# The 64-row last chunk of 704 gated values, filled with zeros to 128 rows in two feed-forward stages

## What is computed

```python
gate = jnp.einsum('bted,edf->btef', dispatched, gate_proj)
up = jnp.einsum('bted,edf->btef', dispatched, up_proj)
acts = jax.nn.silu(gate) * up                                  # 704 gated values
expert_out = jnp.einsum('btef,efd->bted', acts, down_proj)     # sum over 704
```

```python
gate = fp4_linear(x, w_gate)
y = fp4_linear(x, w_up)
h = jax.nn.silu(gate) * y
return fp4_linear(h, w_down)                                   # sum over 704
```

## Time and profile before

| | |
|---|---|
| median of 3 runs | 1807.83 us (1807.45 to 1808.09) |
| the profiled execution, its own time | 1806.81 us |
| its span, from first to last instruction | 1804.9 us |
| mean granted TensorE clock | 0.944 of full speed |
| TensorE matmul busy | 1566.6 us (87%) |
| VectorE, ScalarE, GpSimd busy | 983.1, 487.1, 401.8 us |
| expert stage of layer 0 | about 174 to 502 us |
| dense stage of layer 2 | about 1144 to 1386 us |

### The profile page before, as it was taken

The page is one execution under the profiler, slowest core; times in us unless marked ns, Lnnn a source line. Parts: engine busy times, 40 slices in busy tenths (PEclk is TensorE's granted clock), DMA queues, the critical chain, the costliest instruction groups (busy, mean ns, idle before and its releaser), DMA issues. The chain is left out here.

```text
span 1804.9 us, 33711 instructions
## 1 busy us (share of the span) xinstructions
PE 1566.6 (87%) x11830; PEld 1134.7 (63%) x11830; DVE 983.1 (54%) x2513; ACT 487.1 (27%) x1045; POOL 401.8 (22%) x734
## 2 busy tenths in 40 slices
PE   5878999999968989699978999768888787999992
PEld 3653889898947744355543566445555563799982
DVE  4455334444469957766635433589887456222224
ACT  2331111010156631355522122233322331111100
POOL 0102111111042001111111344323111101344440
PEclk9998999999979999899998999879999999999996
DMA  4104889888821006234305033210000001899995
GB/s 143 38 2 135 299 294 308 292 305 292 262 65 36 2 1 165 94 101 108 86 20 187 21 88 89 73 30 18 1 1 1 1 2 48 275 320 320 314 313 186
DMA packets 162223, 240.64 MB, mean 133 GB/s; under 512 B 19808, under 2 KB 109344, under 8 KB 161984
## 3 DMA queue, kind: packets, MB, share of 16 engines
q1 hardware_dynamic: 149440, 208.35, 35.7%
q0 software_dynamic: 10512, 28.72, 5.8%
q10 hardware_dynamic: 2160, 2.10, 0.3%
HBM read 208.96 MB, written 30.15 MB: 132 GB/s over the span
## 5 line engine op out<-in xcount | busy, mean ns | idle before, releaser
L1543 DVE TENSOR_REDUCE l1a_nm<-l1a_sc 128x1 f32<-128x512 f32 (+3 forms) x256 | 107.2, 482 | 53.7 <-PE l1a_sc L1679 53.7
L2309 PEld LDWEIGHTS e0b_gp<-e0b_xT,e0b_wgu 128*128 128x128 f32 x936 | 107.4, 192 | 14.5 <-issue 12.3
L2309 PE MATMUL e0b_gp<-e0b_xT,e0b_wgu 128*128 128x128 f32 x936 | 114.9, 279 | 1.8 <-DVE e0b_hT L2379 1.3
L2330 PE MATMUL e0b_yp<-e0b_wd,e0b_hT 128*128 128x256 f32 x468 | 115.1, 388 | 0.6 <-issue 0.6
L2360 ACT ACTIVATE e0b_sg<-e0b_gp 128x640 f32<-128x640 f32 x78 | 33.5, 481 | 285.9 <-PE e0b_gp L2309 285.9
L2330 PEld LDWEIGHTS e0b_yp<-e0b_wd,e0b_hT 128*128 128x128 f32 x468 | 82.6, 189 | 21.9 <-issue 13.9
L2309 PE MATMUL e0b_up<-e0b_xT,e0b_wgu 128*128 128x128 f32 x780 | 93.5, 275 | 0.0
L2309 PEld LDWEIGHTS e0b_up<-e0b_xT,e0b_wgu 128*128 128x128 f32 x780 | 90.2, 192 | 0.0
L2309 PE MATMUL e3b_gp<-e3b_xT,e3b_wgu 128*128 128x128 f32 x624 | 77.8, 278 | 6.9 <-DMA e3b_wgu<-in_L_ffn_W 5.5
L2309 PEld LDWEIGHTS e3b_gp<-e3b_xT,e3b_wgu 128*128 128x128 f32 x624 | 73.9, 192 | 15.1 <-DMA e3b_wgu<-in_L_ffn_W 7.3
L2360 ACT ACTIVATE e3b_sg<-e3b_gp 128x512 f32<-128x512 f32 x39 | 23.3, 597 | 206.7 <-PE e3b_gp L2309 206.7
(11 more groups left out here) (606 smaller groups left out, 3530.4 us busy)
## 6 DMA issues: line engine op xcount, KB each, us to landing
e3b_wgu<-in_L_ffn_W SPq DMA_DIRECT2D x78, 512.0 KB, 5.4
e0b_wgu<-in_L_ffn_gate_proj SPq DMA_DIRECT2D x39, 704.0 KB, 4.5
e0b_wgu<-in_L_ffn_up_proj SPq DMA_DIRECT2D x39, 704.0 KB, 5.9
e0b_wd<-in_L_ffn_down_proj SPq DMA_DIRECT2D x39, 640.0 KB, 5.2
e3b_wd<-in_L_ffn_W SPq DMA_DIRECT2D x39, 512.0 KB, 7.1
x_rows<-xn SPq DMA_DIRECT2D x3, 2048.0 KB, 8.6
l_parts<-l1p_split SPq DMA_DIRECT2D x16, 384.0 KB, 3.1
l_stack_k<-l_parts SPq DMA_DIRECT2D x48, 128.0 KB, 2.8
```

Of the source, the lines that this page charges most:

```text
L1543: nc.vector.tensor_reduce(nm[:, g % 2, q, i:i + 1], sc[q], AX_X, ALU.max, negate=True).then_inc(max_done, 1)
L2309: last = nc.tensor.matmul(dst[:, f, :], wgu[j][:, k, at + f * P:at + (f + 1) * P], xT[j][:, k, :], start=(k == 0), stop=(k == KC - 1))
L2330: last = nc.tensor.matmul(yp[:], hT[j][0:FW[f], f, :], wd[j][0:FW[f], f, :], start=(f == 0), stop=(f == FC - 1))
```

## The change

The last chunk of 64 is treated as a full one of 128 whose lower 64 rows hold zeros, in both stages. In `blocks` VectorE clears, once, rows 64 to 127 of the last chunk in both `hT` and both `wd` buffers; the loads and the multiplication go on writing rows 0 to 63 alone. In layer 2 `hq` becomes 768 wide with its last 64 columns cleared once, the lower half of `f2w_down`'s last chunk is cleared once, the sixth transpose is a full one, and ScalarE copies the fifth and sixth chunk in one instruction. TensorE waits once in each stage for the clearing.

```diff
@@ blocks
+            padded = sem("padded")
...
                         for f in range(FC):
-                            last = nc.tensor.matmul(yp[:], hT[j][0:FW[f], f, :], wd[j][0:FW[f], f, :], start=(f == 0),
-                                                    stop=(f == FC - 1))
+                            last = nc.tensor.matmul(yp[:], hT[j][:, f, :], wd[j][:, f, :], start=(f == 0), stop=(f == FC - 1))
...
                     up_product(0, 0)
+                    if LEFT:
+                        pe.wait_ge(padded, 4)
...
+                    for j in range(2 if LEFT else 0):
+                        nc.vector.memset(hT[j][LEFT:P, FULL, :], 0.0).then_inc(padded, 1)
+                        nc.vector.memset(wd[j][LEFT:P, FULL, :], 0.0).then_inc(padded, 1)
                     copy_rows(0, 0)
@@ lookup_and_feed_forward
-                tmp("hq", [P, F]), tmp("hT", [P, FC, P])
+                tmp("hq", [P, FC * P]), tmp("hT", [P, FC, P])
...
                             act.wait_ge(h_turned, n * NG + g + 1)
-                            full = [f for f in chunks if FW[f] == P]
-                            last = nc.scalar.copy(hT[:, full[0]:full[-1] + 1, :], hp[g][:, 0:len(full), :])
-                            for f in chunks:
-                                if FW[f] < P:
-                                    last = nc.scalar.copy(hT[0:FW[f], f, :], hp[g][0:FW[f], f % 4, :])
-                            last.then_inc(h_copied, 1)
+                            nc.scalar.copy(hT[:, chunks[0]:chunks[-1] + 1, :], hp[g][:, 0:len(chunks), :]).then_inc(h_copied, 1)
...
+                    nc.vector.memset(hq[:, F:], 0.0).then_inc(padded, 1)
+                    nc.vector.memset(dT[FW[FC - 1]:P, FC - 1, :], 0.0).then_inc(padded, 1)
...
                             for f in chunks:
-                                last = nc.tensor.transpose(hp[g][0:FW[f], f % 4, :], hq[:, f * P:f * P + FW[f]], ident)
+                                last = nc.tensor.transpose(hp[g][:, f % 4, :], hq[:, f * P:(f + 1) * P], ident)
...
                             for f in chunks:
-                                last = nc.tensor.matmul(yp[:], hT[0:FW[f], f, :], dT[0:FW[f], f, :], start=(f == 0),
-                                                        stop=(f == FC - 1))
+                                last = nc.tensor.matmul(yp[:], hT[:, f, :], dT[:, f, :], start=(f == 0), stop=(f == FC - 1))
...
+                    pe.wait_ge(padded, 2)
                     pe.wait_ge(c_step, B + 3)
```

More of the change, by code:

```diff
@@ L2759, in hidden_job @@
             def hidden_job(n):
-                return (hq[:], h[:], F, h_bufs, h_quant, n)
+                return (hq[:, 0:F], h[:], F, h_bufs, h_quant, n)
             with nc.Block() as block:
```

## The result

The changed kernel took 1792.66 us (median of 6 runs, 1787.31 to 1797.32), the kernel before beside it 1807.64 us (6 runs, 1805.06 to 1809.14): ratio 0.9918, 95% interval 0.9899 to 0.9937, so 0.8% faster, and clear of noise. Two further series of the same kernel gave 0.9934 (0.9913 to 0.9955) and 0.9918 (0.9890 to 0.9946). Forecast were 1790.8 us and a range of 1786.5 to 1795.0 us. The runs of the changed kernel spread over 10 us, and its profiled execution (1797.32 us) is at the upper end. That spread is no mark of the change: in the later series the kernel before spread as far (23 runs from 1801.38 to 1812.51 us, 17 runs from 1801.53 to 1815.75 us).

A forecast was written before the change was run, and what follows sets the result against it. TensorE's chain of passes was taken to bound layer 0's expert stage. Savings of 14.4 us there, 2.5 us in layer 2's down product and 0.1 us in its turns and copies sum to 17.0 us: 1790.8 us, range 1786.5 to 1795.0 us.

The forecast's parts named there:

- The bound: Layer 0's expert stage: TensorE alone sets the time, busy for 60.00 of 60 us, block after block.
- The seams: Layer 0's expert blocks: weight loads wait where the row count changes, about 0.19 us each, 0.38 us a block, 14.4 us.
- The transfers: Layer 0's weight transfers: share rises to 0.944 at 319 GB/s, still under the ceiling; nothing counted for them.
- The latest landing: Layer 0's gate and up weights: latest arrival 7.9 us after issue, against 10.3 us available after the change.
- The rival: Layer 0: weight transfers take back part of the gain, as layer 3's 317 GB/s may be the limit; 1797 us, chance 0.07.
- Clearing: Start of layer 2's stage: two clearings on VectorE cost 0 to 0.5 us, taken as 0; layer 0's are hidden.
- Layer 2's down products: Layer 2: filling saves 0.33 us per down product on the path, 2.5 us in all, bounds 0 and 5.3 us.
- 7 of 16 on the path: Layer 2: 3 + 1 + 2 + 1 down products count at 0.33 us each, plus 0.19 us, making 2.5 us.
- the wait for `xq`: Layer 2, TensorE: a longer wait here that eats the whole saving would show the forecast wrong.
- The two rules: Trainium skill statements: loads overlap matmuls only when row groups differ; changing tiling mode drains TensorE. Both weighed against profile rows.
- The drained columns: Layer 2's 64-column turns: changing columns also drains TensorE, so filling saves 2.7 us more; 1788.1 us, chance 0.03.

The follow-up runs named there:

- the two chunks together and apart: Kernel before, layer 0's down product over four 128-row and two 64-row chunks, the two adjacent (1806.96 us) or separated (1823.26 us).
- five chunks: Changed kernel with the last chunk left out of layer 0's down product, all loads kept: 1773.39 us, ratio 0.9818.

## Why the prediction was right, and where it was off

*The bound.* Right. Layer 0's expert stage follows TensorE alone, in every profile.

*The seams.* Right, in mechanism and size. Forecast were 0.38 us a block, 7.73 us for the block and 14.4 us for the stage; measured 0.39 us, 7.72 us and 14.8 us. The comparison with layer 3 gave the size, and the two chunks together and apart gave the cause: 0 and 0.39 us more with the same loads and passes.

*The transfers.* Right to count nothing, with a wrong ceiling. Forecast were a share of 0.944 and 319 GB/s; measured are 0.95 and 310 GB/s. The share was well foretold and the rate was not, because it rested on one short window: windows of 60 us in this stage read from 292 to 304 GB/s before the change, depending on where they lie. Over 210 to 450 us it was 298 GB/s before and 314 GB/s after, and 298 x 8.11 / 7.72 = 313. The same explains why my rates at full share differed, 338 GB/s for layer 0 and 330 for layer 3: with 298 GB/s at 0.90 layer 0 comes to 331. The latest landing was 7.9 us and is 9.2 us, by the same view of the changed kernel:

```profile
DMA to landing us min/median/max: 4.1/5.6/9.2
```

That is still under the 10.3 us available. It is no sign of tighter transfers: with the chunks together and apart, where blocks are as long as before or longer, the latest landings were 8.9 and 9.1 us, and with five chunks, the shortest blocks, 7.7 us. The rival took layer 3's 317 GB/s as the limit; the five chunks ran at 330 GB/s without a wait.

*Clearing.* The step "I take 0" was wrong. I leaned on a wait of 0.36 us for gathered rows, and on later ones. The cost is 0.58 us in the first pair and about 0.55 us over all profiles, slightly over the upper bound of 0.5 us that I gave. The waits behind the clearings belong to transfers that seem to be issued only as VectorE frees their buffers, so a later VectorE also made them later; I read this from the code, and it was not tested.

*Layer 2's down products.* The forecast of 2.5 us in that stretch came out as 3.7 us in the first pair of profiles, and as some 2 us between kernels with the same mean clock there. But in time the part gave nothing that can be told from 0 (1.0012 and 1.0003 by itself), and the whole stage, which was to be 2 to 3 us shorter, was 1.5 us shorter in the first pair and 0.4 us between two kernels with the same mean clock over it. The term was over-sized in the sum: it should have had the 0.55 us of the clearings against it, and the step from a shorter down product to a shorter stage is not borne out as I counted it (7 of 16 on the path). Which engine takes the time back is open; the wait for `xq` that I named as a possible sign did grow, from 2.8 to 3.9 us. The clock adds to it: the first stretch of the stage took 61.6 to 65.8 us with the same passes.

*The two rules.* The drained columns did not happen. Full loads lie under full passes in the changed kernel too (57.52 us of loads in 60.00 us of passes), against the sentence in the Trainium skill, "TensorE: Matmul & The Clock Gate", section Part 3, by which a load overlaps only when the row group differs. The same section also lets a load go ahead that targets the background weight buffer; the prediction weighed only the one sentence, and with the other one these rows agree. The drain at a change of mode, which the Trainium skill states in "TensorEngine Tiling (Array Packing)", section Tiling Modes, agrees with this case for rows (0.39 us for a change there and back) and does not for columns (0.0 us before 16 loads, and none before the full load behind).

*The total.* Forecast 17.0 us, measured 15.0 us between the medians (11.4 to 18.3 us by the interval of the ratio), with 14.8 us of it in one stage. That the medians fell inside the range is right for the seams and in part luck for the rest: 2.5 us were credited to layer 2, which by itself gave nothing measurable, and 7 of the 16 single runs of the changed kernel lie above the 1795.0 us of my range. What I left out is that a stage which is not touched is not a constant: the stretch from the last expert block to layer 2's first square took 643.2 to 643.8 us in the six kernels with layer 0's timing of before or with it lengthened, and 642.1 to 648.9 us in the eight in which that stage was shortened. The start of layer 0's stage moved by up to 4.2 us as well. This is a term of no sign, of a few us, that belongs into the range. In the first profile it was 5.7 us.

## What to carry to other kernels

Where a stream of TensorE passes bounds a stage, look for the idle time ahead of weight loads by shape: a chunk with fewer rows than its neighbours costs there twice, once in and once out, and zeros in the unused rows remove it at no cost in passes. If a chunk can't be filled, put all chunks of one height side by side. Clear the padding in a wait of the engine that clears, not at the start of a stage, and before crediting 3 us to a small second part, run that part alone. Work that is put in to delay a kernel must stand where its engine does not wait anyway, and the trace must show that the delay arrived.

## What the runs showed of the hardware

- Changing from 128 to 64 rows and back costs 0.39 us of TensorE's time at full clock with passes of float32, whether the 64-row part has two or four passes. Changing the columns of the weight load from 128 to 64 has no such cost.
- Layer 0's DMA queues delivered 331 GB/s at a share of 0.99 over 240 us, in the kernel with five chunks; layer 3's 317 GB/s at 0.96.
- The same instructions between layer 0 and layer 2 took from 642.1 to 648.9 us. The windows show TensorE busy for up to 5 us longer on 1351 equal passes, at a mean granted clock of 0.88 to 0.91, while the busy times of VectorE and ScalarE agree to 0.3 us. What decides about the clock there was not settled.
